# Moving weight low halves and routing weights between GpSimd and VectorE ahead of the expert tiles

## The chip, the core and the metric

The kernel runs on one core of a Trainium2 chip. A core has TensorE (matmul), VectorE, ScalarE and GpSimd, which the profile calls PE, DVE, ACT and POOL, and SyncE (SP), which here issues DMAs. The engines run their own lists of instructions in order and wait for each other at semaphores. The metric is the device time of one execution in microseconds.

## What is computed

A transformer block on x of 2 x 1024 tokens with 256 features: cross attention to a context of 77 rows, added through a tanh gate, and then a mixture of experts (8 experts, top 2 of a router, tokens sorted by expert) plus a shared expert, added through a second gate. Cut to what matters:

```
x = x + tanh(g_xattn[0]) * xattn(layernorm(x), ctx, mask, W, b)
h = layernorm(x)
logits = h @ w_router
top_logits, top_idx = top_k(logits, 2)
scores = softmax(top_logits)
# each token goes to its two experts e:
#   y = (silu(proj) * gate) @ fc2_w[e],  proj, gate = split(h @ fc1_w[e])
moe = (y of both experts * scores).sum()
shared = silu(h @ gate_w) * (h @ up_w) @ down_w
out = x + tanh(g_ffn[0]) * (moe + shared)
```

## The kernel before

Large products are made as three products of a high and a low part: the high part of a number is its rounding to the matmul's type (`hi`), the low part is the rest (`lo`, the number minus its high part). Weights come in 30 chunks of 128 x 512 (6 for the shared expert, 24 for the eight experts). A chunk's high half is written by ScalarE (`cut_hi`), its low half by GpSimd or VectorE (`cut_lo`), in place of the raw chunk. `by_pool` says which: GpSimd has chunks 0 to 6 and the two of `MID`, 12 and 13. VectorE has both halves of chunks 7 to 11 (`BY_DVE`) and the low halves of 14 to 29, in numbers by unit that the table `LATER` gives.

The program has these stages. First come eight groups of 256 tokens: norm, attention, residual, second norm, transpose of h, router. Then the shared expert runs in 16 units (`gate_up`, `silu`, `product`, `silu_hi`, `product_lo`, `down`), numbered 0 to 15, each a quarter of the tokens times a quarter of the 512 hidden features. Two of them, 14 and 15, are held back for the end. Unit n's `down` runs on TensorE two units later.

While these units run, the tokens are sorted. They are routed in two halves of 8 tiles of 128 tokens. For each half VectorE picks the experts (`first_choice`, `second_choice`) and TensorE ranks them (`rank`). VectorE then computes the places in the sorted order (`slots`). GpSimd writes into each row of `hrows`, behind the 256 features of a token, its second expert's mark and two fields of its weight (`weigh`, `weight_fields`, with a tanh on ScalarE between them, `weight_tanh`), and scatters the rows into the DRAM array `rows`, 16 indirect DMAs for each half (`scatter`). When all 32 have landed, SyncE loads tiles of 128 sorted rows, and the 39 expert tiles run on TensorE. Each is a transpose, `m_up`, a transpose and `m_down`. ScalarE scales the result, and GpSimd scatters it into `parts` by the indices `dst`. At the end the parts for the first and second choice come back (`low_buf`, `high_buf`) and VectorE adds them (`add_low`, `add_high`), between the two units held back.

TensorE enters the expert tiles in this order: `gate_up(13)`, transpose of tile 0, `down(11)`, then waits for all low halves, then `m_up` of tile 0.

All orders are written out by hand. Those around the change are GpSimd's list after the last `norm_first` (lines 397 to 428), VectorE's list from `first_choice(0)` on, and ScalarE's `weight_tanh(0)`, which stands behind `silu(1)` and `silu_hi(0)`. On VectorE each unit of the shared expert from 8 on is

```
product(u)
if u % FC == 1:
    add_down(u // FC - 1)
cut_later(u)
product_lo(u)
```

## Time and profile before

| | us |
|---|---|
| median of three runs | 251.15 (250.44 to 251.5) |
| the profiled execution, its own time | 251.19 |
| its span in the trace | 249.3 |
| TensorE busy | 223.9 (90%) |
| VectorE busy | 163.2 (65%) |
| ScalarE busy | 126.9 (51%) |
| GpSimd busy | 126.3 (51%) |

The trace is of one execution, and its times count from the start of its span; 1.9 us of the execution lie around the span. Busy shares are means over all stages. Of the page's 40 slices of 6.2 us, the twentieth is the only one in which TensorE is busy for less than a tenth, and the granted clock of TensorE is lower in this slice and the next than in all others. In the eight slices ahead of it GpSimd is busy for seven to eight tenths of the time, VectorE for six to nine.

### The profile page before, as it was taken

The page shows a single profiled execution, that of the slowest core. Times are in us where ns is not written, and L with a number is a line of the kernel's source. Part 1 is how long each engine was busy: PE and PEld are TensorE (multiplying, and loading weights), DVE is VectorE, ACT ScalarE, POOL GpSimd, SP SyncE. Part 2 cuts the span into 40 slices and gives each one's busy share as a digit, 9 for nine tenths or more (in the row PEclk, how much of TensorE's full clock was granted, in tenths as well). Part 3 has the DMA queues.
Part 4 walks back from the last instruction along what each step waited for, and adds up shares of the span by engine and source line. Part 5 has one row for each costly group of instructions (what it writes and reads, how often), then busy time and mean ns, then how long its engine had stood idle before and what let it go on. Part 6 is the DMA issues. An engine that isn't in the chain of part 4 may idle for free.

```text
span 249.3 us, 5130 instructions
## 1 busy us (share of the span) xinstructions
PE 223.9 (90%) x1373; PEld 194.9 (78%) x1373; DVE 163.2 (65%) x502; ACT 126.9 (51%) x309; POOL 126.3 (51%) x179
## 2 busy tenths in 40 slices
PE   7688999999999999994079999999999999999970
PEld 7567788888888988883078888888888888888850
DVE  1548877778577899992025666665656565664596
ACT  2255877776545534551012565656656565655320
POOL 1968987553588787888300143434343333434600
PEclk9999999999999999999569999999999999999999
DMA  6999910000021154213143334343433323018677
GB/s 177 280 403 408 399 57 3 0 0 3 7 101 67 64 178 143 89 44 107 64 128 90 85 89 125 86 125 90 100 108 103 113 80 102 24 47 252 211 281 307
DMA packets 18114, 32.04 MB, mean 129 GB/s; under 512 B 3030, under 2 KB 9307, under 8 KB 18088
## 3 DMA queue, kind: packets, MB, share of 16 engines
q1 hardware_dynamic: 14160, 22.42, 28.7%
q0 software_dynamic: 3408, 8.46, 9.1%
q10 hardware_dynamic: 520, 0.84, 1.0%
q8 instruction: 13, 0.21, 0.4%
q14 instruction: 13, 0.11, 0.1%
HBM read 19.95 MB, written 12.67 MB: 131 GB/s over the span
## 4 chain that ended last, share of the span: by engine, by line
PE 42%; POOL 9%; issue 6%; DVE 5%; DMA 2%; ACT 1%; SPq 0%; DVEq 0%; POOLq 0%; ACTq 0%
PE bank L922 35%; POOL rows L392 8%; PE bank L1099 4%; PE bank L1119 3%; DVE acc L895 1%; DVE acc L675 1%; DVE act_lo L610 1%; DMA rows<-hrows,slot 1%; DMA hrows<-rows 1%; POOL ew_lo L238 1%; DVE acc L889 0%; ACT act_hi L436 0%; DVE act L662 0%; SPq L275 0%; DVE act L857 0%
## 5 line engine op out<-in xcount | busy, mean ns | idle before, releaser
L424 POOL DMA_INDIRECT parts<-y_out,dst x39 | 39.0, 1000 | 76.0 <-DVE dst L851 72.4
L392 POOL DMA_INDIRECT rows<-hrows,slot x32 | 38.5, 1203 | 11.1 <-issue 11.1
L857 DVE TENSOR_TENSOR act<-act,bank 128x256 f32<-128x256 f32 x39 | 16.4, 421 | 35.0 <-ACT act L559 35.0
L559 ACT ACTIVATE act<-bank 128x256 f32<-128x256 f32 x39 | 15.0, 384 | 38.0 <-PE bank L922 36.3
L922 PE MATMUL bank<-ew_hi,m_xt_hi 128*128 x78 | 30.8, 394 | 0.5 <-DVE m_xt_lo L610 0.5
L922 PE MATMUL bank<-ew_hi,m_xt_lo 128*128 x78 | 30.8, 395 | 0.0
L922 PE MATMUL bank<-ew_lo,m_xt_hi 128*128 x78 | 30.7, 394 | 0.0
L922 PE MATMUL bank<-ht_hi,sw_hi 128*128 128x512 f32 x64 | 25.5, 399 | 0.0
L922 PE MATMUL bank<-ew_hi,act_hi 128*128 x78 | 25.2, 323 | 0.2 <-DVE act_lo L610 0.2
L922 PE MATMUL bank<-ht_lo,sw_hi 128*128 128x512 f32 x64 | 25.1, 391 | 0.0
L922 PE MATMUL bank<-ht_hi,sw_lo 128*128 128x512 f32 x64 | 24.9, 390 | 0.0
L1099 PE MATMUL bank<-ident,hrows 128*128 128x128 f32 x78 | 15.1, 275 | 10.8 <-DMA hrows<-rows 10.8
L610 DVE TENSOR_TENSOR m_xt_lo<-bank,m_xt_hi 128x256 fp32r<-128x256 f32 x39 | 16.2, 415 | 12.1 <-ACT m_xt_hi L436 12.1
L1099 PEld LDWEIGHTS bank<-ident,hrows 128*128 128x128 f32 x78 | 10.9, 142 | 16.2 <-issue 11.2
L436 ACT ACTIVATE act_hi<-act 128x512 fp32r<-128x512 f32 x16 | 10.1, 632 | 25.8 <-DVE act L662 19.5
L922 PE MATMUL bank<-ew_hi,act_lo 128*128 x78 | 21.9, 281 | 0.0
L922 PE MATMUL bank<-ew_lo,act_hi 128*128 x78 | 21.9, 281 | 0.0
L436 ACT ACTIVATE m_xt_hi<-bank 128x256 fp32r<-128x256 f32 x39 | 14.9, 381 | 13.3 <-PE bank L1099 13.3
L922 PE MATMUL bank<-sw_hi,act_hi 128*128 128x256 f32 x64 | 19.1, 299 | 1.8 <-DVE act_lo L610 1.8
L571 ACT ACTIVATE y_out<-bank,w_t 128x256 f32<-128x256 f32 x39 | 18.5, 475 | 4.3 <-DMA parts<-y_out,dst 1.5
L922 PE MATMUL bank<-sw_lo,act_hi 128*128 128x256 f32 x64 | 18.6, 291 | 0.0
L922 PE MATMUL bank<-sw_hi,act_lo 128*128 128x256 f32 x64 | 18.6, 290 | 0.0
(148 smaller groups left out, 588.3 us busy)
## 6 DMA issues: line engine op xcount, KB each, us to landing
ew_raw<-in_chunks SPq DMA_DIRECT2D x12, 512.0 KB, 10.9
hrows<-rows SPq DMA_DIRECT2D x39, 130.0 KB, 2.3
acc<-in_x SPq DMA_DIRECT2D x8, 256.0 KB, 4.4
low_buf<-parts SPq DMA_DIRECT2D x4, 512.0 KB, 6.2
high_buf<-parts SPq DMA_DIRECT2D x4, 512.0 KB, 5.6
sw_raw<-in_chunks SPq DMA_DIRECT2D x3, 512.0 KB, 8.4
out<-acc SPq DMA_DIRECT2D x3, 512.0 KB, 2.9
rows<-pad_rows SPq DMA_DIRECT2D x9, 130.0 KB, 2.1
```

The source lines that it names most:

```text
L238: eng.tensor_tensor(out=lo_, in0=raw_, in1=hi_.bitcast(F32), op=ALU.subtract)\
L392: pool.indirect_dma_start(out=rows, out_offset=bass.IndirectOffsetOnAxis(ap=slot[:, h, k, i:i + 1], axis=0), in_=hrows[:, HT * h + i, :], ...
L424: pool.indirect_dma_start(out=parts, out_offset=bass.IndirectOffsetOnAxis(ap=dst[:, t:t + 1], axis=0), in_=y_out[:, t % SLOTS, :], in_offs ...
L436: return a.activation(out_, in_, ACT.Identity).then_inc(s[name], 1)
L559: a.activation(act[:, p, 0:I], M_H[p][:, 0:I], ACT.Silu).then_inc(s["m_sil"], 1)
L571: a.activation(y_out[:, t % SLOTS, :], M_Y[p][:, 0:D], ACT.Identity, scale=w_t[:, t:t + 1])\
L610: return TT(out_, in_, hi_.bitcast(F32), ALU.subtract).then_inc(s[name], 1)
L675: STT(out=acc[:, i, :], in0=BD[g][j // 2][:, (j % 2) * D:(j % 2) * D + D], scalar=tg[:, 1:2], in1=acc[:, i, :], op0=ALU.mult, op1=ALU.add) ...
L857: TT(act[:, p, 0:I], act[:, p, 0:I], M_H[p][:, I:2 * I], ALU.mult).then_inc(s["m_prod"], 1)
L922: ins = pe.matmul(ps, a, b, start=first and i == 0, stop=last and i == total - 1, skip_group_check=not lone)
L1099: ins = pe.transpose(M_X[:, k * P:(k + 1) * P], hrows[:, i, k * P:(k + 1) * P], ident[:])
L1119: ins = pe.transpose(M_A[:, k * P:(k + 1) * P], act[:, p, k * P:(k + 1) * P], ident[:])
```

## The change

It has seven parts.

- GpSimd no longer cuts the low halves of chunks 12 and 13 between its scatters (`MID` goes). VectorE has them, as the first of its low halves from unit 3 on, and `LATER` is 1, 1, 1, 1, 1, 1, 2, 2, 4, 4 for units 3 to 12 instead of 1, 1, 1, 1, 1, 2, 3, 3, 2, 1.
- The weights of the second half (`weigh(1)`, seven operations on GpSimd between the scatters) become `weigh_second`, four operations on VectorE ahead of `product(4)`.
- The first half's weights (`weigh_first`) have six operations instead of seven. The mark that a row carries is smaller by E = 8 in both halves, so `m_dst` compares it with a new `t_expm`, which is `t_exp` minus 8.
- The first half's `weight_fields` stand ahead of `rstd_second` of the last group, and ScalarE's `weight_tanh(0)` ahead of `silu(1)`.
- The first scatter of the second half also waits for `low_second`, which VectorE raises in `weigh_second`.
- ScalarE's `silu(14)` stands ahead of the y scaling `m_y` of the last expert tile.
- VectorE's `add_low(2)` stands ahead of `product(14)` instead of behind it, and `add_low(3)` ahead of `product_lo(14)`.

```diff
-MID = range(IN_A + 5, IN_A + 7)
-LATER = {3: 1, 4: 1, 5: 1, 6: 1, 7: 1, 8: 2, 9: 3, 10: 3, 11: 2, 12: 1}
+LATER = {3: 1, 4: 1, 5: 1, 6: 1, 7: 1, 8: 1, 9: 2, 10: 2, 11: 4, 12: 4}
...
-            weigh(0)
+            weigh_first()
+            weight_fields(0)
             rstd_second(NG - 1)
-            weight_fields(0)
-            scatter(0, 0, 6)
-            cut_lo(pool, MID[0])
-            scatter(0, 6, HT)
-            weigh(1)
-            scatter(0, HT, HT + 6)
-            cut_lo(pool, MID[1])
-            scatter(0, HT + 6, 2 * HT)
+            scatter(0, 0, 2 * HT)
             weight_fields(1)
             scatter(1, 0, 2 * HT)
...
+            def weigh_second():
+                sl = slice(HT, NT)
+                after(v, "picked", NH)
+                TT(wsm[:, 0, sl], idx[:, 0, sl], idx[:, 1, sl], ALU.is_lt).then_inc(s["wts_second"], 1)
+                TT(wsm[:, 1, sl], mx[:, 0, sl], mx[:, 1, sl], ALU.subtract).then_inc(s["wts_second"], 1)
+                TT(hrows[:, sl, D + 1], idx[:, 0, sl], idx[:, 1, sl], ALU.min).then_inc(s["low_second"], 1)
+                after(v, "wts_second", 2)
+                STT(out=wsm[:, 2, sl], in0=wsm[:, 0, sl], scalar=-0.5, in1=wsm[:, 1, sl], op0=ALU.add, op1=ALU.mult)\
+                    .then_inc(s["wts_second"], 1)
...
             cut_later(3)
+            weigh_second()
             product(4)
...
+            TS(t_expm[:], t_exp[:], -float(E), None, ALU.add).then_inc(s["t_expm"], 1)
...
             add_low(1)
+            add_low(2)
             product(U0)
-            add_low(2)
+            add_low(3)
             product_lo(U0)
-            add_low(3)
```

What this makes of GpSimd's list, from the first half's scatters on. `rows<-hrows,slot` is a scatter, `ew_lo` a low half of a weight, `wsm` the weights of the routing. Before, from the first scatter to the second group of eight:

```order
L392 DMA rows<-hrows,slot 17536x260 x6
L238 TENSOR_TENSOR ew_lo<-ew_raw,ew_hi 128x512
L392 DMA rows<-hrows,slot 17536x260 x2
L361 TENSOR_TENSOR low_first<-idx 128x8
L363 TENSOR_TENSOR wsm<-mx 128x8
L366 TENSOR_SCALAR i_low<-low_first 128x8
L367 TENSOR_SCALAR wsm<-low_first 128x8
L369 TENSOR_TENSOR hrows<-i_low,idx 128x8
L371 TENSOR_SCALAR wsm<-wsm 128x8
L373 TENSOR_TENSOR wsm<-wsm 128x8
L392 DMA rows<-hrows,slot 17536x260 x6
```

Behind these stand the second low half, two more scatters, the fields and the other 16 scatters. Now, from the first half's fields to the end of the scatters (`ve`, `nm`, `rs` and `nb` are the last group's norm):

```order
L376 TENSOR_SCALAR hrows<-wsm,tgh 128x8
L378 TENSOR_SCALAR hrows<-wsm,tgh 128x8
L310 TENSOR_SCALAR ve_107<-mv_105 128x2
L311 TENSOR_SCALAR nm_106<-mv_105 128x2
L314 TENSOR_TENSOR rs_108<-ve_107,half 128x2
L334 TENSOR_TENSOR nb_109<-nm_106,rs_108 128x2
L389 DMA rows<-hrows,slot 17536x260 x16
L376 TENSOR_SCALAR hrows<-wsm,tgh 128x8
L378 TENSOR_SCALAR hrows<-wsm,tgh 128x8
L389 DMA rows<-hrows,slot 17536x260 x16
```

The low halves and the weights between the scatters are gone, so that each half's 16 scatters are one piece, and the fields stand ahead of the norm.

VectorE's list, units 9 to 12 of the shared expert. `act<-act,bank` is a product, `act_lo` its low part, `acc<-bank,tg,acc` the adding of `down`. Before:

```order
L675 SCALAR_TENSOR_TENSOR acc<-bank,tg,acc 128x256 x4
L238 TENSOR_TENSOR ew_lo<-ew_raw,ew_hi 128x512 x3
L610 TENSOR_TENSOR act_lo<-act,act_hi 128x512
L662 TENSOR_TENSOR act<-act,bank 128x512
L238 TENSOR_TENSOR ew_lo<-ew_raw,ew_hi 128x512 x3
L610 TENSOR_TENSOR act_lo<-act,act_hi 128x512
L662 TENSOR_TENSOR act<-act,bank 128x512
L238 TENSOR_TENSOR ew_lo<-ew_raw,ew_hi 128x512 x2
L610 TENSOR_TENSOR act_lo<-act,act_hi 128x512
L662 TENSOR_TENSOR act<-act,bank 128x512
L238 TENSOR_TENSOR ew_lo<-ew_raw,ew_hi 128x512
L610 TENSOR_TENSOR act_lo<-act,act_hi 128x512
```

Now:

```order
L666 SCALAR_TENSOR_TENSOR acc<-bank,tg,acc 128x256 x4
L236 TENSOR_TENSOR ew_lo<-ew_raw,ew_hi 128x512 x2
L601 TENSOR_TENSOR act_lo<-act,act_hi 128x512
L653 TENSOR_TENSOR act<-act,bank 128x512
L236 TENSOR_TENSOR ew_lo<-ew_raw,ew_hi 128x512 x2
L601 TENSOR_TENSOR act_lo<-act,act_hi 128x512
L653 TENSOR_TENSOR act<-act,bank 128x512
L236 TENSOR_TENSOR ew_lo<-ew_raw,ew_hi 128x512 x4
L601 TENSOR_TENSOR act_lo<-act,act_hi 128x512
L653 TENSOR_TENSOR act<-act,bank 128x512
L236 TENSOR_TENSOR ew_lo<-ew_raw,ew_hi 128x512 x4
L601 TENSOR_TENSOR act_lo<-act,act_hi 128x512
```

Units 9 and 10 have two low halves each instead of three, units 11 and 12 four each instead of two and one.

VectorE's list in the last stage, before:

```order
L889 TENSOR_TENSOR acc<-acc,low_buf 128x1024 x2
L662 TENSOR_TENSOR act<-act,bank 128x512
L889 TENSOR_TENSOR acc<-acc,low_buf 128x1024
L610 TENSOR_TENSOR act_lo<-act,act_hi 128x512
L889 TENSOR_TENSOR acc<-acc,low_buf 128x1024
L662 TENSOR_TENSOR act<-act,bank 128x512
L895 TENSOR_TENSOR acc<-acc,high_buf 128x1024
L610 TENSOR_TENSOR act_lo<-act,act_hi 128x512
```

Now:

```order
L893 TENSOR_TENSOR acc<-acc,low_buf 128x1024 x3
L653 TENSOR_TENSOR act<-act,bank 128x512
L893 TENSOR_TENSOR acc<-acc,low_buf 128x1024
L601 TENSOR_TENSOR act_lo<-act,act_hi 128x512
L653 TENSOR_TENSOR act<-act,bank 128x512
L899 TENSOR_TENSOR acc<-acc,high_buf 128x1024
L601 TENSOR_TENSOR act_lo<-act,act_hi 128x512
L899 TENSOR_TENSOR acc<-acc,high_buf 128x1024 x3
```

The third low add stands ahead of the product of unit 14, and the fourth ahead of its low part.

## Rows read from the trace of the kernel before

**Rows 1.** Waits of the whole span: line, releaser, us, times, longest.

```profile
PE bank L1099 <- DMA hrows<-rows: 10.8, 1, 10.8
```

**Rows 2.** Windows: length, busy per engine (PE, PEld, DVE, ACT, POOL), clock, DMA, GB/s.

```profile
95.00:115.20 20.20, 20.20 (x115) 17.43 (x113) 17.57 (x32) 10.73 (x20) 16.52 (x12) 1.00 0.23 81
...
118.00:119.00 1.00, 0.00 (x0) 0.00 (x0) 0.00 (x0) 0.00 (x0) 0.70 (x2) 0.89 0.27 92
```

**Rows 3.** The chain of waits after 120 us: start, us, what.

```profile
120.24 2.64 DMA rows<-hrows,slot
...
126.03 0.66 PE bank L1099 x2
126.69 2.53 PE bank L922 x12
...
134.79 1.43 PE bank L922 x12
```

**Rows 4.** Timeline of GpSimd: start, us, line, operation, count, [idle before].

```profile
63.05 0.19 POOL L336 TENSOR_TENSOR nb<-nm,rs 128x2 f32<-128x2 f32 x1
64.64 0.68 POOL L380 TENSOR_SCALAR hrows<-wsm,tgh 128x8 f32<-128x8 f32 x1 [1.40 <-ACT wsm L504]
...
66.63 1.26 POOL L392 DMA_INDIRECT rows<-hrows,slot  x1 [1.02 <-issue]
...
74.27 1.32 POOL L238 TENSOR_TENSOR ew_lo<-ew_raw,ew_hi 128x512 fp32r<-128x512 f32 x1
75.76 0.99 POOL L392 DMA_INDIRECT rows<-hrows,slot  x1 [0.17 <-issue]
77.06 1.18 POOL L392 DMA_INDIRECT rows<-hrows,slot  x1 [0.30 <-issue]
...
81.55 1.07 POOL L392 DMA_INDIRECT rows<-hrows,slot  x1 [0.68 <-issue]
...
92.66 1.13 POOL L392 DMA_INDIRECT rows<-hrows,slot  x1 [0.30 <-issue]
...
95.33 1.06 POOL L392 DMA_INDIRECT rows<-hrows,slot  x1 [0.85 <-issue]
...
99.53 0.98 POOL L392 DMA_INDIRECT rows<-hrows,slot  x1 [0.30 <-issue]
...
103.39 2.89 POOL L392 DMA_INDIRECT rows<-hrows,slot  x1 [0.30 <-issue]
106.59 2.70 POOL L392 DMA_INDIRECT rows<-hrows,slot  x1 [0.31 <-issue]
109.60 2.10 POOL L392 DMA_INDIRECT rows<-hrows,slot  x1 [0.30 <-issue]
...
120.24 0.98 POOL L392 DMA_INDIRECT rows<-hrows,slot  x1 [0.31 <-issue]
```

**Rows 5.** The page's groups of instructions: the scatters of the token rows.

```profile
L392 POOL DMA_INDIRECT rows<-hrows,slot x32 | 38.5, 1203 | 11.1 <-issue 11.1
```

**Rows 6.** Timeline of VectorE before the hole, columns as in 4.

```profile
88.91 1.98 DVE L811 TENSOR_SCALAR turns_f<-down,cum 128x4 f32<-128x4 f32 x2
...
98.98 1.28 DVE L238 TENSOR_TENSOR ew_lo<-ew_raw,ew_hi 128x512 fp32r<-128x512 f32 x2
...
102.95 1.88 DVE L238 TENSOR_TENSOR ew_lo<-ew_raw,ew_hi 128x512 fp32r<-128x512 f32 x3
...
108.96 1.28 DVE L238 TENSOR_TENSOR ew_lo<-ew_raw,ew_hi 128x512 fp32r<-128x512 f32 x2
...
111.16 0.69 DVE L662 TENSOR_TENSOR act<-act,bank 128x512 f32<-128x512 f32 x1 [0.32 <-PE bank L922]
...
115.34 0.69 DVE L662 TENSOR_TENSOR act<-act,bank 128x512 f32<-128x512 f32 x1 [1.40 <-PE bank L922]
```

**Rows 7.** Timeline of VectorE in the last stage.

```profile
235.84 0.69 DVE L662 TENSOR_TENSOR act<-act,bank 128x512 f32<-128x512 f32 x1 [1.72 <-PE bank L922]
...
239.31 0.68 DVE L662 TENSOR_TENSOR act<-act,bank 128x512 f32<-128x512 f32 x1
```

More of the change, by code:

```diff
@@ L175, in build @@
         t_exp = sb("t_exp", [P, N_TILES])
+        t_expm = sb("t_expm", [P, N_TILES])
         t_w = sb("t_w", [P, N_TILES], I32)
@@ L192, in build @@
             xt_ps xt xp_ps xp sc_ps sc_in sc_max sc_exp eT_ps eT mt_ps s_inv coef resid stats2 mean2 pre2 pow2 rstd2 h_ready
-            hT_ps ht_h ht_l lg_ps lg_read rt picked rank_ps placed wts w_sign w_tanh fields slots scattered pads tb tiles_known
+            hT_ps ht_h ht_l lg_ps lg_read rt picked rank_ps placed wts wts_second low_second w_sign w_tanh fields slots t_expm scattered pads tb tiles_known
             chunk_h chunk_lp chunk_lv gate_ps up_ps chunk_hv sil prod act_h act_l dn_ps dn_added
@@ L386, in scatter @@
                 after(pool, "h_ready", HT * (h + 1))
-                after(pool, "fields", 3 * (h + 1))
+                after(pool, "fields", 3 if h == 0 else 5)
+                after(pool, "low_second", h)
                 after(pool, "const_r", 6)
@@ L593, in _ @@
             m_a(N_TILES - 1, (N_TILES - 1) % 2)
-            for t in (N_TILES - 2, N_TILES - 1):
-                m_y(t, t % 2)
+            m_y(N_TILES - 2, N_TILES % 2)
             after(a, "aT_ps", N_TILES)
-            after(a, "y2_ps", N_TILES)
-            for n in range(U0, UNITS):
-                silu(n)
-                silu_hi(n)
+            silu(U0)
+            m_y(N_TILES - 1, (N_TILES - 1) % 2)
+            silu_hi(U0)
+            silu(U0 + 1)
+            silu_hi(U0 + 1)
             after(a, "dn_added", TOK // P - 2)
@@ L729, in cut_later @@
             def cut_later(u):
-                mine = range(MID.stop, CHUNKS)
+                mine = range(BY_DVE.stop, CHUNKS)
                 first = sum(m for w, m in LATER.items() if w < u)
@@ L847, in m_dst @@
                 v.wait_ge(tile_in[i], 16 * (t // LOADS + 1))
-                TS(dst_tmp[:, t:t + 1], hrows[:, i, D + 1:D + 2], t_exp[:, t:t + 1], float(TOK),
+                after(v, "t_expm", 1)
+                TS(dst_tmp[:, t:t + 1], hrows[:, i, D + 1:D + 2], t_expm[:, t:t + 1], float(TOK),
                    ALU.not_equal, ALU.mult).then_inc(s["dst_t"], 1)
```

43 lines of the change are left out of this document (20 added, 23 removed).

## The prediction

> **What bounds the kernel now.** I first read the table of waits, for the one large hole on TensorE: its first transpose of a gathered tile of tokens waited 10.8 us for that tile to land [rows 1]. The windows show what lies around the hole: 20.20 us busy of 20.20 before it, so that TensorE is the bound there, and a granted clock that falls inside it [rows 2]. The chain of waits names the cause: GpSimd's last scatter starts at 120.24, its rows land, SyncE loads the first tile, TensorE starts at 126.03 [rows 3]. From the last scatter's start to TensorE's restart there are 5.79 us, and from its end (120.24 + 0.98) 4.81. TensorE itself had stopped at about 115.2. So every us by which the row of scatters ends earlier is a us of the hole, until the row ends before 115.2 - 4.8 = 110.4. From there TensorE is the bound again, and it needs all low halves of the weights by then.
>
> GpSimd's timeline shows why the row is so long [rows 4]. Its 32 scatters are busy for 38.5 us [rows 5]. An undisturbed one takes 0.97, and the gap to the next is 0.30, a step of 1.27. So 38.5 - 32 x 0.97 = 7.5 us are delay. Three of them carry most of it: 2.89, 2.70 and 2.10 us are 1.92 + 1.73 + 1.13 = 4.8 us too much. VectorE's timeline shows what runs beside them [rows 6]: low halves and `act_lo`, subtractions with both inputs in SBUF, back to back, 0.60 us each. The run that begins at 102.95 has three low halves and an `act_lo`, and ends at about 105.4; the scatter of 103.39 ends at 106.28, which is 0.97 after 105.31. The run of 108.96 (two low halves and `act_lo`) ends at about 110.8; the scatter of 109.60 ends at 111.70, 0.97 after 110.73. The scatter of 106.59 does the same with the run between these. I read it as a lock: a scatter that starts inside such a run waits for its end. But the scatter of 99.53 started inside the run of 98.98 and lost nothing. So four runs of three or four operations held a scatter three times.
>
> **The change part by part.** GpSimd's list first.
> (a) One low half leaves the row in each half. The first starts at 74.27, as the sixth scatter ends, and the next scatter starts at 75.76, 1.49 later instead of 0.30: saves 1.2. The other one, in the second set of eight, alike: 1.2.
> (b) The second half's weights leave. From 78.24 (77.06 + 1.18) to the next start at 81.55 there are 3.31 instead of 0.30: saves 3.0. With (a) 5.4.
> (c) The first half's weight fields move ahead of the last norm. They had waited 1.40 for ScalarE's tanh [rows 4], which stood behind a silu and a high half and now stands ahead of both. With the tanh done at about 61.0 (my estimate: the weights it reads were ready before the norm began) the two field operations take 0.7, and the norm's four operations 1.6, so it ends at 63.5 instead of 63.24. The first scatter comes about 0.9 later (before: 1.02 after the fields), at 64.4 instead of 66.63: 2.2 earlier. The norm's 0.3 delay ScalarE, which at that time has a high half before it; without that cover it would be 0.3 on TensorE.
> If no delay changed, the row would end 5.4 + 2.2 = 7.6 earlier.
>
> VectorE's list.
> (d) Four operations on 128x8 come in for the second half's weights, about 0.2 each, 0.9 in all; they lie beside TensorE's units of 4.18 us (115.34 - 111.16, [rows 6]). If VectorE had no room there they would cost 0.9.
> (e) The two `turns_f` operations took 1.98 [rows 6] beside GpSimd's second low half. Their neighbours of that size take 0.15, so they should take 0.3: 1.7 back, which brings VectorE into step before unit 8. `t_expm` adds 0.2.
> (f) 18 low halves instead of 16: units 8, 9 and 10 have one less each, unit 11 two more, unit 12 three more. From product 9 on VectorE waits for TensorE's units, so product 11 comes at 111.16 - 4.18 = 106.98, and its run, four low halves at 0.60 and `act_lo`, lies from 107.6 to 110.7. Unit 12's lies from 111.8 to 114.85. Units 9 and 10 have runs of three, 101.6 to 103.4 and 104.0 to 105.9. All low halves are done by 114.3, before TensorE asks for them after 115.2, so this costs TensorE nothing; if that cover went, each late one would cost 0.6.
>
> Now I walk the row again. First half: 64.4 + 16 x 0.97 + 15 x 0.30 = 84.4, and with 1.0 of small delays 85.4 (7.5 less the three long ones leaves 2.7 for all 32). Between the halves there are 1.54 (from 92.66 + 1.13 to 95.33) with the fields in it: 86.9. The twelfth scatter of the second half starts at 86.9 + 11 x 1.27 + 0.9 = 101.8, inside unit 9's run. If all runs hold, the last five start at 101.8 (held, ends 104.4), 104.7 (held, 106.8), 107.1, 108.4 (held, 111.6) and 111.9 (held, 115.8). If one of the first three runs lets its scatter through, the last one stands one place earlier and ends by 111.6, and TensorE restarts at 116.4. A run holds three times in four, so all four hold with 0.32 only, and the first three with 0.42. That is why I take 111.6. Small delays of 1.3 more or less shift everything by one place; both are kept for the range.
>
> Restart at 116.4 instead of 126.03 gives 9.6. With TensorE idle since 115.2, the granted clock averaged 0.89 from 118 to 119 [rows 2]: within that us, near 118.8, it fell from 1.00 (2.4 GHz) to 0.50 (1.2 GHz), 3.6 us into the hole. A hole of 1.2 us should not lose it. What the low clock cost: the first twelve products after the hole took 2.53 us, the same twelve of the next unit but one 1.43 [rows 3], 1.1, and with the transposes, 0.66 for two, I take 1.4. Sum 11.0, at least 9.6 if the clock falls all the same.
>
> (g) The tail. Product 14 waits 1.72 for TensorE [rows 7]; one low add of 1.14 moves into that hole. Product 15 stood behind an add until 239.31, though its gate and up need only 4.18 - 1.43 = 2.75 us after those of unit 14: 235.84 + 2.7 = 238.5. Gain 0.8, if the high parts have landed that much earlier; if not, 0. On ScalarE the last y scaling moves behind a silu, which delays the last y scatter by about 1 us; only the output's DMAs wait for it, and these come after the last adds: 0.
>
> Sum, against the profiled execution of 251.19 us (0.04 above the median, so the same): 251.19 - 11.0 - 0.8 = **239.4 us**.
>
> **A rule against the rows.** In the rows the lock outlasts the borders between operations: the scatter of 103.39 passed three of them. The Trainium skill, SBUF — State Buffer, section "Who interferes with whom", says that a VectorE instruction with two SBUF inputs contends with a GpSimd instruction that reads SBUF, and that the ports are held for one whole instruction. By that a scatter loses one operation at most, 0.6 us, and the row ends before 110.4: the skill's rule leads to rival A, 238.2 us. No chance or price below rests on this paragraph.
>
> **Rivals.**
> A: two or more of the runs let their scatter through, and the row ends before 110.4. The hole is gone: 251.2 - 10.8 - 1.4 - 0.8 = 238.2. For it: the scatter of 99.53. Against: the three others.
> B, the forecast: 239.4.
> C: all four hold and the row ends at 115.8. Restart 120.6, 5.4 earlier; a hole of 5.4 us outlasts the 3.6 after which the clock fell, so the 1.4 stay lost: 251.2 - 5.4 - 0.8 = 245.0. Should only unit 12's run let its scatter through, about 241.
> C': small delays put one more scatter behind it, which starts at 116.1: restart 121.9, 246.3.
> D, slower: the long scatters come not from VectorE but from the scatters themselves, when more than six follow each other without other work; the long ones are the seventh to ninth of such a row, and now both halves are rows of 16. If the last ten of each took (2.89 + 2.70 + 2.10) / 3 = 2.56, that is 20 x 1.59 = 32 us instead of the 4.8 now, less 7.6: some 19 slower, 270. It decides from five such scatters more than now. Against it: the row is back at 0.98 by 120.24 [rows 4], and each long one ends by a run.
> E: VectorE falls behind and its late runs move to TensorE's entry into the tiles, so that the hole stays under another name: 250.
>
> **How the numbers follow.** B 0.35, A 0.22, C 0.26 and its variant at 241 0.07, C' 0.07, D 0.01, E 0.02. The range leaves out C', D and E, with a few tenths at each end: 237.8 to 245.5. B's own range is 238.8 to 241. A measurement of this kernel can tell about 0.5% (1.3 us) from no change. All but D and E are faster by more: 0.97, same 0.02, slower 0.01.
>
> **What would show it.** The first scatter near 64.4 and the second half's first near 87; no scatter over 1.5 us before 101; two or three of 1.5 to 3.2 us after it, each ending 0.97 after a run of VectorE; the last ending at 111.6 (B), before 110.4 (A) or at 115.8 (C); TensorE's hole at 1.2, 0 or 5.4 us, its clock at 1.00 throughout in A and B; `turns_f` at 0.3. I would be wrong if scatters are long away from VectorE's runs, if GpSimd waits for slots or fields between the halves, or if TensorE waits for VectorE in units 9 to 13.

## The result: slower by 1.7% where it was timed, and 4% faster on another chip

| | before | after |
|---|---|---|
| median of 4 executions | 250.8 us (250.3 to 251.5) | 255.6 us (253.9 to 257.4) |
| ratio | | 1.017, 95% interval 1.011 to 1.024 |
| forecast | | 239.4 us, range 237.8 to 245.5 |

The change made the kernel slower, and the forecast missed by 16 us. The same unchanged kernel took 241.2 us on a chip that came up in the experiments, where the kernel before took 252.6 (ratio 0.958, interval 0.951 to 0.964). So this section reads the trace of the slower execution, and the trace of that other chip comes with the experiments. The profiled execution of after took 257.38 us, its span is 255.5. All ratios here and below rest on the executions within 1.5% of their kernel's fastest; where a kernel's executions spread further, their range is given.

What was forecast for GpSimd came, up to the end of the first half's scatters. The first scatter starts at 64.41 (forecast 64.4), the sixteenth ends at 85.36 (forecast 85.4). No scatter takes over 1.33 us, and the 38.5 us of [rows 5] are 32.9. From there it is no longer as forecast. GpSimd's timeline (start, duration, line, operation, in brackets the idle time before and its releaser):

```profile
64.41 1.26 POOL L389 DMA_INDIRECT rows<-hrows,slot  x1 [0.83 <-issue]
...
84.31 1.05 POOL L389 DMA_INDIRECT rows<-hrows,slot  x1 [0.30 <-issue]
88.94 0.35 POOL L376 TENSOR_SCALAR hrows<-wsm,tgh 128x8 f32<-128x8 f32 x1 [3.58 <-ACT wsm L496]
89.28 0.32 POOL L378 TENSOR_SCALAR hrows<-wsm,tgh 128x8 f32<-128x8 f32 x1
92.92 1.32 POOL L389 DMA_INDIRECT rows<-hrows,slot  x1 [3.32 <-DVE slot L728]
...
113.04 0.98 POOL L389 DMA_INDIRECT rows<-hrows,slot  x1 [0.30 <-issue]
```

It waits 3.58 us for ScalarE's tanh and 3.32 for VectorE's slots. The second half starts at 92.92 instead of 86.9. Even so its row ends at 114.02, 7.2 us earlier than before [rows 4], and the 10.8 us of [rows 1] are gone: no wait of TensorE for a tile is left in the trace. The time is lost elsewhere. The windows (length, busy time of PE, PEld, DVE, ACT and POOL with counts, granted clock, DMA share, GB/s) show it in two places, where before TensorE was busy throughout [rows 2]:

```profile
80.00:84.00 4.00, 2.44 (x14) 2.04 (x12) 0.78 (x2) 0.52 (x2) 3.09 (x4) 1.00 0.28 100
84.00:88.00 4.00, 2.20 (x17) 1.72 (x17) 0.51 (x1) 0.48 (x1) 1.05 (x2) 0.65 0.18 67
88.00:92.00 4.00, 4.00 (x18) 3.23 (x16) 3.71 (x11) 3.18 (x8) 0.66 (x2) 0.50 0.00 0
...
104.00:108.00 4.00, 2.50 (x10) 1.32 (x8) 1.44 (x4) 0.65 (x2) 3.09 (x4) 1.00 0.36 125
108.00:112.00 4.00, 1.84 (x6) 1.38 (x7) 1.29 (x2) 0.98 (x2) 3.09 (x4) 0.64 0.41 140
112.00:116.00 4.00, 2.60 (x7) 1.34 (x6) 0.00 (x0) 0.01 (x1) 1.71 (x2) 0.50 0.28 100
116.00:120.00 4.00, 4.00 (x12) 3.22 (x13) 3.34 (x7) 4.00 (x8) 0.00 (x0) 0.58 0.39 82
```

The reader is to see three things. TensorE is busy for 2.4 and 2.2 us of 4 at 80 to 88, and for 2.5, 1.8 and 2.6 of 4 at 104 to 116. GpSimd is busy with scatters in the same windows. And the clock goes from 1.00 to 0.50, which is 1.2 instead of 2.4 GHz, within each of the two stretches and stays there behind it: in 88 to 92 TensorE is busy all the time and gets 18 matmuls done, where the execution on the other chip has 25. The idle pieces of 0.2 us and more add up to 8.1 us in 60 to 125, none longer than 1.1.

Hardly any of this is a wait for another engine's work. The table of waits calls them "issue", and calls much of the other engines' waiting "remote", which stands for a releaser that the trace does not name:

```profile
PEld bank L926 <- issue: 14.5, 20, 1.2
ACT act_hi L427 <- remote: 14.1, 3, 7.0
DVE act L653 <- remote: 9.6, 2, 4.8
```

TensorE's own rows show what the pieces are. These are five matmuls in a row of one `down`, with no wait on any semaphore between them:

```profile
83.84 0.28 PE L926 MATMUL bank<-sw_lo,act_hi 128*128 128x256 f32 x1 [0.91 <-issue]
84.56 0.37 PE L926 MATMUL bank<-sw_hi,act_lo 128*128 128x256 f32 x1 [0.45 <-issue]
85.96 0.37 PE L926 MATMUL bank<-sw_hi,act_hi 128*128 128x256 f32 x1 [1.02 <-issue]
86.67 0.58 PE L926 MATMUL bank<-sw_lo,act_hi 128*128 128x256 f32 x1 [0.33 <-issue]
87.05 0.41 PE L926 MATMUL bank<-sw_hi,act_lo 128*128 128x256 f32 x1
```

The first four start 0.7 or 1.4 us apart, where such matmuls start 0.12 apart at full clock. Of the 8.1 us, 7.8 lie ahead of matmuls that wait for nothing. So TensorE is held between its own instructions, with its work at hand.

The other engines feel it in a second way. An engine tells the others that an instruction is done by raising a semaphore; this increment is what I call its report. One late report can be read from rows. The last matmul of unit 2's `down` starts on TensorE at 78.27 and takes 0.28. ScalarE's `silu_hi(4)` needs it and VectorE's `product(4)`. The rows of PE, DVE and ACT:

```profile
78.27 0.28 PE L926 MATMUL bank<-sw_hi,act_lo 128*128 128x256 f32 x1
...
83.22 0.69 DVE L653 TENSOR_TENSOR act<-act,bank 128x512 f32<-128x512 f32 x1 [4.83 <-remote]
...
87.52 0.63 ACT L427 ACTIVATE act_hi<-act 128x512 fp32r<-128x512 f32 x1 [7.00 <-PE bank L926]
```

ScalarE stands still for 7.00 us. `product(4)` is done at 83.91, and from there ScalarE waits until 87.52 only for a matmul that had ended at 78.55: the trace has the increment at 87.44, 9 us late. VectorE's wait of 4.83 is of the same kind: the increment for its gate and up, done at 77.12, stands at 83.12. Late increments are seen from 10 us into the first row of scatters and from 6 us into the second, until 2 us after each. All that are recorded late are TensorE's; none is of another engine. With ScalarE and VectorE held, the tanh, and with it the fields, and the slots come late. VectorE's `product(13)` stands at 132.67 instead of 115.34 [rows 6].

### The profile page after: what moved, and what is told of

The parts are those of the page before. It is cut to its first block, busy times and chain, and to the rows that moved or that the text cites. A ratio compares the mean times of both kernels' runs of the same rounds, so it can differ in the third digit from the quotient of the medians.

```text
span 255.5 us, 5161 instructions
## 1 busy us (share of the span) xinstructions
PE 231.7 (91%) x1373; PEld 198.8 (78%) x1373; DVE 162.6 (64%) x509; ACT 126.6 (50%) x309; POOL 115.4 (45%) x169
## 4 chain that ended last, share of the span: by engine, by line
PE 75%; DVE 7%; DMA 6%; issue 5%; ACT 4%; POOL 1%; SPq 1%; DVEq 0%; POOLq 0%
PE bank L926 58%; PE bank L1103 3%; PE bank L982 3%; PE bank L1123 3%; DMA high_buf<-parts 3%; DVE acc L633 2%; DMA acc<-in_x 2%; ACT s_in L463 2%; DVE st L639 2%; PE bank L1003 1%; PE bank L1001 1%; PE bank L991 1%; DMA parts<-y_out,dst 1%; ACT xp L456 1%; DVE s_max L618 1%
## 5 line engine op out<-in xcount | busy, mean ns | idle before, releaser
L389 POOL DMA_INDIRECT rows<-hrows,slot x32 | 32.9, 1029 | 13.3 <-issue 10.0
L926 PE MATMUL bank<-ht_hi,sw_hi 128*128 128x512 f32 x64 | 27.1, 423 | 0.1
L926 PE MATMUL bank<-ht_hi,sw_lo 128*128 128x512 f32 x64 | 26.5, 415 | 0.7 <-issue 0.7
L926 PE MATMUL bank<-ht_lo,sw_hi 128*128 128x512 f32 x64 | 26.6, 416 | 0.1
L601 DVE TENSOR_TENSOR act_lo<-act,act_hi 128x512 fp32r<-128x512 f32 x16 | 11.0, 690 | 15.5 <-ACT act_hi L427 13.5
L653 DVE TENSOR_TENSOR act<-act,bank 128x512 f32<-128x512 f32 x16 | 11.0, 685 | 12.4 <-remote 9.6
L601 DVE TENSOR_TENSOR act_lo<-bank,act_hi 128x256 fp32r<-128x256 f32 x39 | 16.5, 424 | 1.6 <-ACT act_hi L427 1.0
L926 PEld LDWEIGHTS bank<-ew_hi,m_xt_lo 128*128 128x128 f32 x78 | 14.7, 188 | 3.3
```

The costliest lines, as they stand in the source:

```text
L389: pool.indirect_dma_start(out=rows, out_offset=bass.IndirectOffsetOnAxis(ap=slot[:, h, k, i:i + 1], axis=0), in_=hrows[:, HT * h + i, :], ...
L601: return TT(out_, in_, hi_.bitcast(F32), ALU.subtract).then_inc(s[name], 1)
L653: TT(act[:, n % 2, :], act[:, n % 2, :], GU[n % 2][1][:], ALU.mult).then_inc(s["prod"], 1)
L926: ins = pe.matmul(ps, a, b, start=first and i == 0, stop=last and i == total - 1, skip_group_check=not lone)
```

## The experiments

The theories. R: it is the scatters, at the rate at which GpSimd now issues them, that hold up TensorE and its reports. V: VectorE's new order or its late low halves. O: what was moved ahead of the last norm, or the tail. The kernels ran in five sittings on four chips, called A, B, C and D here; the ratios are to the kernel before in the same sitting. The expectations bring in further letters for theories of their own, each explained there.

### First sitting, chip A: parts of the change, and a row with stops

**Only the low halves leave GpSimd** (on before):

```diff
-MID = range(IN_A + 5, IN_A + 7)
-LATER = {3: 1, 4: 1, 5: 1, 6: 1, 7: 1, 8: 2, 9: 3, 10: 3, 11: 2, 12: 1}
+MID = range(IN_A + 5, IN_A + 5)
+LATER = {3: 1, 4: 1, 5: 1, 6: 1, 7: 1, 8: 1, 9: 2, 10: 2, 11: 4, 12: 4}
...
-            cut_lo(pool, MID[0])
...
-            cut_lo(pool, MID[1])
```

> The kernel before with one part of the change: no low halves on GpSimd between scatters (VectorE cuts all 18, by the table of after); weights, fields and tail as before. GpSimd's scatters now come as 8, weights, 8, fields, 16. Theory R (long unbroken rows of scatters hold up the other engines, TensorE's reports of finished work first): the row of 16 stalls TensorE after its 7th or 8th scatter, about 8 us lost near 105 to 116 as in the kernel after, which lost them there; the rows of 8 lose 0 to 2 us; the time is 252 to 257. Rival V (the late lows or the weights on VectorE are the cause): with the lows' table alone VectorE would be late and TensorE would wait for products that VectorE is still busy ahead of; 252 to 256 too, but VectorE would show no idle time of over 1 us between 82 and 112. Rival O (the cause lies in what is done ahead of the last norm or in the tail, not here): 248 to 250, TensorE busy up to 112.

Measured: 1.007 (1.001 to 1.013), on four of ten executions; the ten took 251.2 to 258.4 us, with 256.1 in the middle, against 251.4 for the kernel before. The trace is of one of 255.8. In it TensorE stands still in 14 pieces between 90 and 114, 7.8 us in all. VectorE has waits of 2.0, 3.9 and 6.2 us in the same stretch, so it is not late, as V would have it: it is held too.

**Only the second weights move to VectorE** (on before):

```diff
-            weigh(1)
...
+            def weigh_second():
+                sl = slice(HT, NT)
+                after(v, "picked", NH)
...
             cut_later(3)
+            weigh_second()
```

> The kernel before with the other part alone: the second half's weights on VectorE (five operations instead of four, for the same result), GpSimd's two low halves left in place. GpSimd's scatters come as 6, low, 8, low, 2, fields, 16. Theory R: the row of 8 costs 0 to 2 us; the row of 16 is held by VectorE's lows as before, so no stall of TensorE; the end of the row comes about 2 us earlier, 248 to 250.5. Rival V by the weights: VectorE late by 1 us in unit 4 and tanh late, slots later than 85.1; 251 to 253. Rival O: 248 to 250.

Measured: 0.993 (0.987 to 0.998), on five of ten executions that took 247.9 to 255.0; the trace is of the longest. A stall of 1.8 us at 86 and shorter ones up to 119, 5.4 us together, though both low halves are on GpSimd and VectorE's table is the old one. This is a miss: I had expected VectorE's low halves to hold the second row's scatters, and none took over 1.37 us.

**GpSimd's low halves back, and with them VectorE's old table of low halves** (on after):

```diff
-LATER = {3: 1, 4: 1, 5: 1, 6: 1, 7: 1, 8: 1, 9: 2, 10: 2, 11: 4, 12: 4}
+MID = range(IN_A + 5, IN_A + 7)
+LATER = {3: 1, 4: 1, 5: 1, 6: 1, 7: 1, 8: 2, 9: 3, 10: 3, 11: 2, 12: 1}
...
-            scatter(0, 0, 2 * HT)
+            scatter(0, 0, 6)
+            cut_lo(pool, MID[0])
+            scatter(0, 6, HT + 6)
+            cut_lo(pool, MID[1])
+            scatter(0, HT + 6, 2 * HT)
```

> The kernel after with GpSimd's two low halves back between the first half's scatters, and VectorE's table of before; everything else as after. Rows 6, low, 8, low, 2, then 16. Theory R: the stall of TensorE at 82 to 87 goes (slots again near 85 instead of 91.9), fields near 85; the row of 16 stalls TensorE only if VectorE's lows do not hold the scatters; 240 to 246 if they hold it, 248 to 252 if not. Rival V by the weights, O by the fields ahead of the norm: the stalls stay, 254 to 257.

Measured: 0.987 (0.975 to 0.999), on three of six executions that took 247.8 to 252.5; the trace is of the longest. Stalls at 83 to 89 and 103 to 114, 6.0 us. The first row's, which I had expected to go, are still there: two breaks of 1.2 to 1.6 us in it do not do.

**Two stops in each row** (on after), until all scatters so far have landed:

```diff
                 for n in range(n0, n1):
                     k, i = n % 2, n // 2
+                    if n in (5, 10):
+                        pool.wait_ge(s["scattered"], 16 * (2 * HT * h + n))
```

> The kernel after with nothing but two stops in each half's row of scatters: ahead of the 6th and the 11th, GpSimd waits until all scatters so far have landed (some 2 us each, by the 2.4 to 4.9 us from issue to landing of before). GpSimd executes nothing more; VectorE's order is untouched. Theory R: rows of 5, 5 and 6, no stall of TensorE in either half; slots near 85; the second half's row runs from 89 to 113 at most, so the tiles start then and the time is 238 to 244. Rivals V and O: VectorE's work and the fields are as in after, so the stalls stay and the stops make the row 4 us longer, 255 to 260.

Measured: 1.002 (0.996 to 1.007), with executions from 249.9 to 256.1; the trace is of the longest. This was a miss in the time and a hit in the cause. All stalls are gone, with VectorE's list untouched, so V and O fall. But the four stops cost GpSimd 10.2 us, and the row ends at 124.6, so that TensorE waits for its first tile again. Two waits and two windows of it:

```profile
PE bank L1105 <- DMA hrows<-rows: 11.6, 1, 11.6
POOL rows L391 <- DMA rows<-hrows,slot: 10.2, 4, 3.2
```

```profile
84.00:88.00 4.00, 4.00 (x37) 3.50 (x36) 3.22 (x11) 0.63 (x1) 2.91 (x3) 1.00 0.18 67
...
108.00:112.00 4.00, 4.00 (x25) 3.51 (x24) 4.00 (x7) 2.79 (x5) 3.39 (x3) 1.00 0.19 69
```

### Second sitting, chip C: the same kernels, and no stalls

> The kernel before, unchanged, in the same sitting as the others, for its trace: in its first trace no stall of TensorE stood ahead of 115 us and three scatters took 2.1 to 2.9 us. If the stalls belong to what the change does, its trace shows none again. If they come with any row of scatters in some executions (rival M, two courses of the same program: either scatters are held, or TensorE's products), this trace may show stalls of TensorE at 84 to 112 and no scatter over 1.5 us, with a time of 252 to 254 instead of 250.

> The kernel after, unchanged, in the same sitting: 253 to 257, TensorE's stalls at 82 to 87 and 105 to 117 again. Under M one run in some would show none and take about 250.

Measured: the kernel before as ever (0.997, interval 0.993 to 1.001). The kernel after 241.2 us (240.3 to 242.2), ratio 0.958 (0.951 to 0.964). I had not expected this. Its trace, windows and GpSimd's timeline:

```profile
84.00:88.00 4.00, 4.00 (x25) 3.52 (x24) 3.76 (x13) 1.64 (x3) 2.95 (x4) 1.00 0.18 67
...
108.00:112.00 4.00, 4.00 (x24) 3.51 (x24) 3.52 (x7) 1.23 (x2) 1.46 (x2) 1.00 0.19 69
112.00:116.00 4.00, 4.00 (x25) 3.45 (x24) 3.51 (x7) 1.62 (x3) 0.00 (x0) 1.00 0.35 99
```

```profile
85.17 0.36 POOL L376 TENSOR_SCALAR hrows<-wsm,tgh 128x8 f32<-128x8 f32 x1
85.52 0.82 POOL L378 TENSOR_SCALAR hrows<-wsm,tgh 128x8 f32<-128x8 f32 x1
87.19 1.06 POOL L389 DMA_INDIRECT rows<-hrows,slot  x1 [0.85 <-POOL hrows L378]
...
104.04 1.50 POOL L389 DMA_INDIRECT rows<-hrows,slot  x1 [0.30 <-issue]
...
108.41 1.35 POOL L389 DMA_INDIRECT rows<-hrows,slot  x1 [0.30 <-issue]
```

TensorE is busy from 60 to 217 with no gap of over 0.2 us, at full clock. The fields and the slots are ready when GpSimd comes, as forecast. ScalarE's operation that stood at 87.52 stands here right behind the product that it needs, which ended at 78.49:

```profile
78.59 0.63 ACT L427 ACTIVATE act_hi<-act 128x512 fp32r<-128x512 f32 x1 [1.22 <-PE bank L926]
```

The two traces differ in one more thing. The trace has a record of each increment, and in the one of the slower execution 112 of 1170 such records are missing; here none. All traces fall into two kinds: between 110 and 138 are missing in those of chips A and B and in that of after (44 in one), 0 to 8 in those of C and D and in the first trace of before. I call A and B chips of the first kind. So the traces of before and after that the result stands on are of two kinds.

**A window of four scatters** (on after):

```diff
+                    m = 2 * HT * h + n
+                    if m >= 4:
+                        pool.wait_ge(row_out[m % 4], 16 * (m // 4))
```

> The kernel after, with each scatter waiting until the one four ahead of it has landed (four counters in turn). At 1.28 us a step and 2.4 us from issue to landing the wait costs nothing unless landings are late. Theory Q (a backlog of outstanding transfers holds up the other engines): the wait holds the row as soon as there is one, the stalls of TensorE shrink to under 2 us, the time is 240 to 250. Theory R (the rate at which GpSimd issues scatters): landings are in time, the wait never holds, the time stays 253 to 257.

Measured on chip C: 0.959 (0.953 to 0.964), which tells nothing apart there.

**A small operation between any two scatters** (on after):

```diff
+                    if n > n0:
+                        pool.tensor_scalar(spare[:, 2 * HT * h + n, :], e_reg[:], 1.0, 1.0, ALU.mult, ALU.add)
```

> The kernel after with one small GpSimd operation (128x8, about 0.35 us) between any two scatters, whose result nobody reads: steps of 1.5 us instead of 1.28. Theory R: TensorE's stalls shrink to under half of the 13 us between 82 and 117, slots come at 85 to 88, the row ends near 113 to 115, the time is 242 to 250. Theory Q: no change but a longer row, 254 to 258, since a step of 1.5 us still lets a backlog of 4 us grow. Rival V (VectorE's order): the stalls stay at full size too.

Measured on chip C: 0.987 (0.981 to 0.992). The steps of 1.42 us and more scatters held by VectorE end the row 7.5 us later than in after, and TensorE waits 6.5 us for its first tile.

### Third sitting, chip A again: the four of the second

> The kernel before once more, to meet another chip. Theory C (the chip decides: on some chips TensorE is held up while GpSimd scatters, and the trace lacks over 100 of some 1150 reports of finished work; on others neither is seen): on a chip of the first kind the trace of before has missing reports and stalls of TensorE between 80 and 112, yet the same time, 250 to 253, because TensorE waits for the tiles until 126 in any case; on the other kind 250 to 253 with no stall. Theory W (the order in which before runs keeps it free of stalls on every chip): no stall of TensorE on either kind.

Measured: 0.999 (0.996 to 1.003). 128 reports are missing, yet there is no stall. The wait for the tile stands where it always stood, and the window is full:

```profile
PE bank L1099 <- DMA hrows<-rows: 9.3, 1, 9.3
```

```profile
84.00:88.00 4.00, 4.00 (x25) 3.55 (x24) 3.12 (x10) 1.46 (x4) 3.09 (x4) 1.00 0.30 109
```

So theory W holds and not C in its first form: TensorE is not held in the order of before on a chip of the first kind either. But its increments come late there too: twelve records between 76 and 107 us stand 0.4 to 3.0 us after the last matmul that can have made them, where the traces of before from the other kind have none. They cost TensorE no idle time.

> The kernel after once more. Theory C: 253 to 257 with stalls where the other traces of this sitting lack reports, 240 to 242 where they lack none; nothing between. Theory S (one program falls into one course or the other by chance, on one chip too): times of both kinds in one sitting.

Measured: 1.022 (1.018 to 1.026), 255.5 to 256.1. Nothing between 242.2 and 253.9 was seen in twelve executions of this kernel, in three sittings. As far as these go, the chip decides and not chance (S falls).

> The kernel after with each scatter waiting until the one four ahead has landed. On a chip without stalls it took 241.9. On a chip with stalls, theory Q (a backlog of outstanding transfers holds TensorE) gives 241 to 248, the waits holding GpSimd; theory R (the rate of scatters, whatever has landed) gives 253 to 257.

Measured: 1.019 (1.010 to 1.028), with executions from 254.1 to 258.5. The stalls stay as they are:

```profile
84.00:88.00 4.00, 2.35 (x8) 1.63 (x8) 0.56 (x1) 0.72 (x2) 1.19 (x2) 0.57 0.18 67
...
108.00:112.00 4.00, 2.00 (x8) 1.35 (x9) 1.29 (x2) 0.00 (x0) 3.08 (x4) 0.99 0.33 118
```

The wait on the scatter four ahead held GpSimd nowhere for more than its usual 0.3 us. So no transfers pile up, and Q falls.

> The kernel after with a small GpSimd operation between any two scatters, steps of some 1.45 us in place of 1.28. On a chip without stalls it took 248.7, since the row of scatters ends 2.2 us after the other's and TensorE waits from 115 to 122. On a chip with stalls, theory R gives shorter stalls and 247 to 251; theory Q leaves them, 254 to 258.

Measured: 0.995 (0.991 to 0.999), with executions from 247.9 to 252.0, and no stall. On chip A a usual step of 1.28 us (in after's first row 1.33 in the mean) holds TensorE up, and one of 1.42 (here 1.54 in the mean) does not. Six increments are still late, by up to 3.1 us. Its 7.6 us of idle time are a wait for the tile:

```profile
PE bank L1106 <- DMA hrows<-rows: 7.6, 1, 7.6
```

```profile
84.00:88.00 4.00, 4.00 (x25) 3.55 (x24) 2.77 (x10) 0.41 (x1) 3.45 (x6) 1.00 0.28 100
```

### Fourth sitting, chip B: how much, where and of what

**The operation ahead of every second scatter:** `if n % 2 == 0 and n > n0:` in the diff above.

> The kernel after with the small GpSimd operation ahead of every second scatter only: steps of 1.28 and 1.42 in turn, 1.35 in the mean. Theory R with a sharp limit between 1.28 and 1.42 us a step: on a chip with stalls some 2 to 6 us of stalls are left, 246 to 252; on a chip without, the row ends 1 to 4 us after the kernel after's, 241 to 245. Theory P (what helps is any work between scatters, the mean step does not matter): no stall left on either chip, 243 to 246.

Measured: 0.972 (0.966 to 0.978), with executions from 243.2 to 248.9, and 2.0 us of stalls, all at 83 to 86. The first row's steps are 1.41 in the mean. The second row is free of stalls; in it VectorE's runs hold some scatters, and its mean step is 1.53:

```profile
84.00:88.00 4.00, 2.71 (x6) 1.83 (x7) 1.03 (x2) 1.28 (x3) 2.62 (x4) 0.70 0.28 100
...
108.00:112.00 4.00, 4.00 (x25) 3.51 (x24) 3.55 (x7) 2.27 (x4) 3.35 (x4) 1.00 0.28 100
```

**The operation in the first row alone:** `if h == 0 and n > n0:`.

> The kernel after with the small operation between the first half's scatters alone. Theory R: on a chip with stalls those at 81 to 87 go (slots near 85, fields near 89), those of the second row stay, some 8 us of lost time with the clock's half speed: 248 to 252; on a chip without, the first row ends at 88.5 instead of 85.2, the second starts 3 us later and TensorE just waits for nothing or up to 2 us: 241 to 244.

Measured: 0.989 (0.987 to 0.992). Each row's stalls answer to its own rate:

```profile
84.00:88.00 4.00, 4.00 (x36) 3.46 (x36) 2.74 (x10) 1.06 (x2) 3.39 (x7) 1.00 0.27 100
...
108.00:112.00 4.00, 2.37 (x11) 1.32 (x10) 3.17 (x7) 1.84 (x4) 3.11 (x3) 1.00 0.29 100
```

**Half the bytes** (on after): each scatter writes 128 of a row's 260 columns. The tiles then hold 128 new columns and old fields, and the results go to places in sequence, so its time is read only up to the tiles.

```diff
-                        in_=hrows[:, HT * h + i, :], in_offset=None, bounds_check=PAD_ROW - 1, oob_is_err=False,
+                        in_=hrows[:, HT * h + i, 0:D // 2], in_offset=None, bounds_check=PAD_ROW - 1, oob_is_err=False,
```

> The kernel after with scatters that carry 128 of the 260 columns: as many scatters and rows, half the bytes (the tiles then hold 128 columns and fields of other tokens, and the tokens' results go to places in sequence; the time is to be read up to the tile loop). Theory R in issues (each scatter's row list and reports load the path): on a chip with stalls TensorE stalls at 81 to 87 and 105 to 117 as in after. Rival B (the bytes that the scatters move, some 100 GB/s, hold TensorE): no stall or under a third of it. On a chip without stalls it tells nothing apart.

Measured: 1.000 (0.996 to 1.005), on five of eight executions that took 249.7 to 258.7. With 33 GB/s in the window in place of after's 67, TensorE is as short of work as there:

```profile
84.00:88.00 4.00, 2.25 (x14) 1.55 (x13) 1.09 (x2) 0.63 (x2) 0.97 (x1) 0.69 0.10 33
```

So in the first row it is not the bytes: 2.9 us of stalls, 3.4 in after, and a scatter's usual step is 1.28 as with all columns. The second row had only 1.5 us of them, 4.7 in after, but its steps were longer too, 1.42 against 1.34 in the mean. B falls as the sole cause; a part for the bytes is not ruled out.

**One stop in each row** (on after): `if n == 8:` in the diff of the two stops.

> The kernel after with one stop in each row, ahead of its 9th scatter, until the first eight have landed (2.4 us or more). Theory R: eight scatters in a piece at 1.28 us stay under what the other engines can stand (the first trace of after showed TensorE's first stall 17 us after the row began): no stall, slots near 85, first row to 88, second from 89 to 116, 243 to 247 on either kind of chip. If a backlog of eight is already too many, 2 to 6 us of stalls on the chip with stalls, 248 to 252.

Measured: 0.974 (0.968 to 0.980). No stall; the times of its five executions lie between 243.5 and 251.7. In the profiled one, the longest, the stop shifted the row against VectorE's runs of four low halves, and two scatters were held by whole runs. GpSimd's timeline:

```profile
109.40 3.31 POOL L391 DMA_INDIRECT rows<-hrows,slot  x1 [0.30 <-issue]
113.01 3.30 POOL L391 DMA_INDIRECT rows<-hrows,slot  x1 [0.30 <-issue]
```

### Fifth sitting, chip D: is one version good on both kinds?

> The small operation ahead of every second scatter in both rows, again, in the hope of the other kind of chip. On a chip without stalls (no reports missing from the trace): the first row ends at 86.4 instead of 85.2, the second 1 to 3 us after the kernel after's 109.8, TensorE waits 0 to 3 us for the first tile, 241 to 244. On a chip with stalls: 244 to 246 as before.

Measured: 242.6 us (241.0 to 246.3), ratio 0.962 (0.957 to 0.967), on a chip that misses 8 reports. With 0.972 on chip B this one version beats the kernel before on both kinds; on the first kind it is some 5% ahead of the kernel after (1.022, on chip A; the two have not run on one chip), on the other kind it loses about 1 us to it (0.958).

> The small operation between any two scatters of the first row, ahead of every second one in the second. Theory R: on a chip with stalls none is left in the first row, which ends near 89; the second starts near 90.5 (the alternate one's started at 91.2, late by its stalls), so its end and the time are the same, 243 to 246, with TensorE's lost time in one wait for the first tile instead of in stalls. On a chip without stalls it is 2 us slower than the alternate one, 243 to 246.

Measured: 0.977 (0.973 to 0.981), 3.5 us behind the alternate one: TensorE waits 4.5 us for the first tile, not 1.6. On the first kind it has not run.

| | A or B, over 40 records missing | C or D, at most 8 missing |
|---|---|---|
| after | 1.022 (A) | 0.958 (C) |
| window of four | 1.019 (A) | 0.959 (C) |
| operation between all | 0.995 (A) | 0.987 (C) |
| every second | 0.972 (B) | 0.962 (D) |
| all in the first row, every second in the other | not run | 0.977 (D) |
| one stop a row | 0.974 (B) | not run |

## Why the prediction was wrong

**Right on both kinds of chip**: (a), (b) and (c), since the first scatter came at 64.41 and 64.33 for 64.4, and the first row ended at 85.36 and 85.12 for 85.4. (e): the two `turns_f` took 0.36 and 0.49 instead of 1.98. (d): the weights on VectorE cost TensorE nothing on chip C.

**The step that failed** is the walk of the second half's row, "Between the halves there are 1.54 with the fields in it: 86.9", and behind it the sentence that every us by which the row ends earlier is a us of the hole. Both take TensorE's, VectorE's and ScalarE's lists as they stood and ask only when GpSimd is done. What a faster row costs the engines beside it was put at nothing, without a reason. On a chip of the first kind it slows the lists beside it: the fields came at 88.94 and the second row at 92.92, and TensorE lost 8.1 us in pieces and ran at half clock from inside each group of them on. Against the execution on chip C, whose `product(13)` stands at 115.39, after's stands at 132.67: 17.3 us, and the times differ by 257.38 - 240.27 = 17.1. Up to that product TensorE is idle for 8.4 us more and busy for 8.9 more. Its clock was at 0.50 from 85.2 to 92.0 and from 109.1 to 119.3, and it was busy for 13.2 us of that, so the half clock explains at most 6.6 of the 8.9 (an estimate: half of 13.2). The other 2.3 lie in stretches that the trace shows as busy, and what they are is not shown.

My list of what would prove me wrong had it: "if GpSimd waits for slots or fields between the halves". Rival D came closest, and it got a chance of 0.01: long unbroken rows of scatters do the harm. But D looked for it in the scatters, which were undisturbed (1029 ns in the mean), and it hit TensorE. Its price was wrong as well, 19 us instead of 5. Nor is it an unbroken number that counts: a row with eight in a piece between breaks of 1.2 to 1.6 us stalled, unbroken rows of sixteen at 1.42 did not. What spoke for it in the trace of before was that its scatters are slow for most of the time: 38.5 us busy [rows 5], with low halves, weights and held scatters between them. I read all of that as loss. The order of before, with a mean step of 1.72 and 1.61 us in its two rows on chip A, and the paced kernels say that part of it was pace.

**On chip C** the row can be held against the forecast. The second row started at 87.19 (forecast 86.9) and ended at 109.76, before 110.4: that is rival A. VectorE's timeline there:

```profile
107.02 0.69 DVE L653 TENSOR_TENSOR act<-act,bank 128x512 f32<-128x512 f32 x1 [1.13 <-PE bank L926]
107.62 2.49 DVE L236 TENSOR_TENSOR ew_lo<-ew_raw,ew_hi 128x512 fp32r<-128x512 f32 x4
```

`product(11)` stands at 107.02, forecast 106.98, and the run of four low halves begins as forecast at 107.6. The scatter of 108.41 starts inside it and takes 1.35. It ends at 109.76, which is 0.97 after 108.79, near the border of the second and third low half: it was held for one operation. The scatters of 102.60 and 104.04 took 1.13 and 1.50. The same kind of run held the scatter of 109.40 of the one-stop kernel for 3.31, to 0.97 after the whole run's end at 111.74. So both happen, as they did in before [rows 4, 6]. My frequency of three in four was no rule, and here it was none in three. What decides between the two stays open. The Trainium skill, SBUF — State Buffer, section "SBUF: two separate sides", has the shared ports held for one whole instruction: the scatter of 108.41 agrees, the one of 109.40 does not.

The 241.2 us of chip C lie in the forecast's range, though not by the forecast's path: the hole was gone as in rival A, and a tail that ran longer than thought hid a part of the gain.

**The tail, (g),** was mis-sized on both kinds of chip. I count it from the end of TensorE's last tile product ahead of the held units to the span's end: 249.3 - 230.14, some 19.1 us, in before, 255.5 - 235.22 = 20.3 in after, 20.5 on chip C. It was to gain 0.8 and lost 1.2 and 1.4. That also closes the account of rival A: its 238.2 was 240.27 on chip C, 0.8 for the gain that did not come and 1.4 for the loss. The high adds of VectorE and the writes of the output from SyncE, of before and then of after:

```profile
241.65 3.49 DVE L895 TENSOR_TENSOR acc<-acc,high_buf 128x1024 f32<-128x1024 f32 x3
246.85 0.33 SPq L295 DMA_DIRECT2D out<-acc  x1
```

```profile
247.42 2.51 DVE L899 TENSOR_TENSOR acc<-acc,high_buf 128x1024 f32<-128x1024 f32 x2 [0.22 <-DMA high_buf<-parts]
248.50 1.58 SPq L291 DMA_DIRECT2D out<-acc  x3
251.65 0.33 SPq L293 DMA_DIRECT2D out<-acc  x1
```

The forecast gain of VectorE is real: in nine of the fourteen traces with this tail (the one with half the bytes left out) the last high add ends 14.2 to 14.3 us into the tail, in before 15.0. In after and on chip C it ends at 14.7 and 15.1, since the last high parts land late there. The loss stands behind the adds. The last write of the output is issued 1.7 us after them and lands 2.0 us later in before, 3.5 in after and 3.3 on chip C. The term that was put at 0 is there: the delayed last y scatter holds the writes of the output, which begin 13.3 us into the tail instead of 11.6 and crowd up to the last one. But that this is what slows the last write is not shown. It took 2.5 to 4.7 us in the fourteen traces, and 2.0 to 2.2 in four of the five with the tail of before, but 4.2 in the fifth (the weights alone on VectorE), whose tail took 21.3. The fourteen tails took 18.8 to 21.1. So the order of the list alone does not settle it, and the cause stays open.

## What to carry to other kernels

A row of indirect DMAs on GpSimd can have a price beside the row: where it runs at its full rate next to a busy TensorE, look in the trace for "issue" pieces on TensorE and for waits on work that ended long before, and try to pace the row when they appear. Here one small operation in every second gap took back some 5% on the chips with stalls and cost about 1 us on the others. Before a wait or another engine's piece of work is booked as loss, ask what it paces. And time a change that packs one engine tighter on more than one chip: 4% faster and 2% slower were the same program.

## What the runs showed of the hardware

- Two kinds of chip. Alike for the kernel before (medians 250.7 to 252.6 in all sittings), they differ by 14 us for the kernel after. The mark in the trace is the missing records: 110 to 138 of some 1170 increments on A and B (44 with half the bytes), 0 to 8 on C and D. Records of landed DMAs are missing in the same traces, 1683 to 2004 of some 2545 being there.
- Late increments are a second mark. Between 60 and 130 us, every trace of the first kind has 6 to 16 recorded increments of TensorE that stand more than 0.25 us after the last matmul that can have made them, and the traces of the other kind have none. In the four traces of this kind without stalls (before, paced, two stops, one stop) the latest is 3.0 to 4.0 us late, in the nine with stalls 5.0 to 14.0. So pacing shortens the delay and does not end it, and the order of before has it too, at no cost in TensorE's time.
- Where TensorE is held, its instructions start some 0.70 to 0.72 us apart, or twice that, though most of them wait for nothing. Between 60 and 115 us each of the nine traces with stalls has 3 to 12 pairs of starts 0.69 to 0.74 us apart, each of the other eleven none. What sets this beat no run shows.
- The limit, with 128 rows a scatter, lies between usual steps of 1.28 and 1.42 us: at 1.28 TensorE was held, at 1.31 and 1.38 in turn 2.0 us of stalls were left in the first row (B, mean 1.41), at 1.42 none (A, mean 1.54). Neither the mean of a row nor the longest piece without a break sorts all rows: one of mean 1.51 with eight in a piece stalled (A), one of mean 1.48 with a stop in the middle did not (B).
- What it is that holds TensorE stays open: the scatters' lists of rows, their own 16 reports each, or the recording of the trace. No run here tells these apart. The recording is the rival to weigh most, because each execution timed here has a recorded span and clock; whether one without recording would stall was not tried. The Trainium skill, NOTIFIC — the notification-queue block, section "Overflow: three behaviours, one of which stalls the engine", says that the block which writes such records can drop one when its queue is full or stall the engine that produced it. That would give missing records and stalls from one cause; the traces agree in that missing records, late increments and stalls come on the same chips, but the kernel before and the paced ones have the first two without the third, and no run shows the cause.
- VectorE's runs can hold a scatter for a whole run of five operations (3.31 us) or for one (1.35), with the same operations in the run.
